# A gated attention and mixture-of-experts kernel: the running maximum is spread by transfers instead of matmuls, and two row normalizations change engine

## The reference, cut to what matters

```python
ig = (ifg @ igate_w.T + igate_b).T
fg = (ifg @ fgate_w.T + fgate_b).T
cs = jnp.cumsum(jax.nn.log_sigmoid(fg), axis=1)
log_D = jnp.where(tril, cs[:, :, None] - cs[:, None, :], -inf) + ig[:, None, :]
max_log_D = jnp.max(log_D, axis=-1, keepdims=True)
D_mat = jnp.exp(log_D - max_log_D)
C = einsum('hsd,htd->hst', qh, kh) / 8 * D_mat
normalizer = jnp.maximum(jnp.abs(C.sum(-1, keepdims=True)), jnp.exp(-max_log_D))
h = einsum('hst,htd->hsd', C / (normalizer + EPS), vh)
x = x + tanh(g_xattn[0]) * layernorm(h) * ln_scale
xn = layernorm(x)
top2 of softmax(xn @ router_w.T); y = weighted experts(xn); s = silu(xn @ sg) * (xn @ su) @ sd
x = x + tanh(g_ffn[0]) * (y + s)
```

## Time and profile before

| | us |
|---|---|
| runs (3) | 1070.31, 1074.41, 1075.37 |
| the profiled execution's own time | 1070.1 |
| its span, first to last instruction | 1068.5 |
| PE, DVE, ACT, POOL busy | 959.1, 807.3, 424.7, 419.4 |
| first stage, to the first expert tile | about 605 |
| mean granted TensorE clock | 0.956 |

### The profile page before, as it was taken

The page is one execution under the profiler, slowest core; times in us unless marked ns, Lnnn a source line. Parts: engine busy times, 40 slices in busy tenths (PEclk is TensorE's granted clock), DMA queues, the critical chain, the costliest instruction groups (busy, mean ns, idle before and its releaser), DMA issues.

```text
span 1068.5 us, 21065 instructions
## 1 busy us (share of the span) xinstructions
PE 959.1 (90%) x6143; PEld 804.3 (75%) x6143; DVE 807.3 (76%) x1995; ACT 424.7 (40%) x957; POOL 419.4 (39%) x315
## 2 busy tenths in 40 slices
PE   3689999999999998988998399999999999999982
PEld 2569888988898886977777278888888888677761
DVE  2887889888988989898866576666666666555885
ACT  2654445444544554444522134444444444332110
POOL 5010211221122122222123827668667777104775
PEclk9989999999999999999958699999999999999996
DMA  7570201220122022111004475576677674915888
GB/s 253 209 311 2 80 31 51 80 79 21 61 80 80 10 72 81 60 60 41 11 31 158 139 227 178 178 231 186 179 212 214 177 213 150 335 70 153 261 291 260
DMA packets 92778, 147.26 MB, mean 138 GB/s; under 512 B 10720, under 2 KB 51168, under 8 KB 91776
## 3 DMA queue, kind: packets, MB, share of 16 engines
q0 software_dynamic: 17872, 65.02, 18.8%
q1 hardware_dynamic: 62896, 59.79, 17.9%
q10 hardware_dynamic: 11904, 21.11, 5.6%
HBM read 89.26 MB, written 56.62 MB: 137 GB/s over the span
## 4 chain that ended last, share of the span: by engine, by line
PE 69%; DVE 13%; issue 7%; DMA 5%; POOL 4%; ACT 1%; SPq 1%; DVEq 0%; POOLq 0%; ACTq 0%
PE bank L1282 19%; PE bank L1152 13%; PE bank L1301 9%; PE bank L1165 5%; PE bank L1075 4%; POOL w_ring L699 3%; PE bank L1007 3%; PE bank L1096 2%; PE bank L1097 2%; PE bank L1349 2%; PE bank L1099 2%; DMA x2n<-routed_x 2%; PE bank L1292 2%; DMA base_out<-in_x_dram 2%; PE bank L1125 1%
## 5 line engine op out<-in xcount | busy, mean ns | idle before, releaser
L1282 PE MATMUL bank<-w_ring,x2nT 128*128 x948 | 254.3, 406 | 13.9 <-DVE x2nT L1864 13.6
L1282 PEld LDWEIGHTS bank<-w_ring,x2nT 128*128 128x128 f32 x948 | 173.8, 191 | 51.5 <-issue 15.8
L1152 PE MATMUL bank<-x2nT,w_ring 128*128 128x256 f32 x1152 | 149.8, 286 | 0.0
L580 POOL DMA_INDIRECT routed_x<-x2n,slot_u x64 | 65.8, 1029 | 204.4 <-DVE slot_u L1625 189.5
L1152 PEld LDWEIGHTS bank<-x2nT,w_ring 128*128 128x128 f32 x1152 | 142.3, 190 | 0.3
L1301 PE MATMUL bank<-w_ring,sh_actT 128*128 x474 | 121.2, 391 | 3.5 <-DVE sh_actT L1853 3.5
L1853 DVE TENSOR_TENSOR sh_actT<-bank,sh_actT 128x256 fp32r<-128x256 f32 x79 | 33.6, 425 | 108.9 <-ACT sh_actT L922 108.9
L1301 PEld LDWEIGHTS bank<-w_ring,sh_actT 128*128 128x128 f32 x474 | 88.8, 188 | 24.0 <-issue 4.6
L662 POOL TENSOR_TENSOR w_ring<-area,one 128x3072 fp32r<-128x3072 f32 x14 | 74.2, 5303 | 81.4 <-PE bank L1301 81.4
L699 POOL DMA_INDIRECT w_ring<-routed_y,y_slot x64 | 66.9, 1046 | 78.0 <-DMA routed_y<-cs_in 52.9
L665 POOL TENSOR_TENSOR w_ring<-area,w_ring 128x3072 fp32r<-128x3072 f32 x14 | 95.9, 6849 | 2.5 <-POOL w_ring L662 2.5
(11 more groups left out here) (224 smaller groups left out, 1959.1 us busy)
## 6 DMA issues: line engine op xcount, KB each, us to landing
x2n<-routed_x SPq DMA_DIRECT2D x316, 64.0 KB, 2.6
routed_y<-cs_in ACTq DMA_DIRECT2D x79, 256.0 KB, 3.3
base_out<-in_x_dram SPq DMA_DIRECT2D x16, 512.0 KB, 5.1
cs_in<-in_ctx_dram SPq DMA_DIRECT2D x16, 512.0 KB, 4.0
area<-n_L_ffn_expert_gate_dram POOLq DMA_DIRECT2D x16, 512.0 KB, 5.2
area<-in_L_ffn_expert_up_dram POOLq DMA_DIRECT2D x16, 512.0 KB, 6.9
area<-n_L_ffn_expert_down_dram POOLq DMA_DIRECT2D x16, 512.0 KB, 8.4
out_dram<-base_out SPq DMA_DIRECT2D x32, 256.0 KB, 3.8
```

Of the source, the lines that this page charges most:

```text
L580: pool.indirect_dma_start(out=routed_x, in_=x2n[:, b.par, j, :], in_offset=None, out_offset=bass.IndirectOffsetOnAxis(ap=slot_u[:, b.par, ...
L1152: last = mm(gu_bank(b.n, m)[:, at:at + S], w[:, w_part, c, m * P:(m + 1) * P], x2nT[:, x_part, c, :], start=(c + p == 0), stop=(c == DC - ...
L1282: last = mm(bank[2 + t.par][:, :], xtT[:, x_part, t.par, c * P:(c + 1) * P], w_gu[:, bass.ds(slot, 1), w_part, c, :].rearrange("p a i -> p ...
```

## The change

The maximum no longer passes through TensorE. SP writes `max_row` (8 rows of 256) to memory, and reads two heads' rows back into all 128 partitions of a new tile `max_spread` (two buffers of one pair each; the second block of 128 queries stands there twice, to be masked for the last 128 keys and left as it is for the first 128). POOL sets what lies above the diagonal to 1e30 by an `affine_select`, one for each pair of heads. ScalarE reads the exponential's input from `max_spread` instead of PSUM. `spread`, `max_hi`, the split in three parts and their constants go. The two banks MB become a second pair of score banks.

The normalized rows `xn` and `x2n` are made by ScalarE as `scale * x + shift` with two operands per partition; DVE makes the small tile of shifts (`-mean * rstd`) instead of the rows. In DVE's order `stats`, `top`, `choose`, `rank`, `slots` and `weigh` move; in PE's order the score pairs move ahead and `rank` behind. POOL's scatter moves behind the masks. The zeros and `kept_w` are written in 4 and 6 pieces of 1 MB from step 5 on, in between SP's other work. Constants and tables that are no longer needed go, and two small tables share another tile.

```diff
-        TP, SM, MB, QK, HO, FF = bank[0], bank[1], bank[2:4], bank[4:6], bank[6], bank[7]
+        TP, SM, QK, HO, FF = bank[0], bank[1], (bank[4:6], bank[2:4]), bank[6], bank[7]
...
+            def max_store(b):
+                sp.wait_ge(row_step.sem, row_step.upto(b.n, 4))
+                sp.dma_start(max_rows[b.par], max_row[:, :]).then_inc(max_out.sem, 16)
+
+            def max_load(b, q):
+                k, lap = q % 2, b.n * 2 + q // 2
+                sp.wait_ge(max_out.sem, max_out.upto(b.n))
+                sp.wait_ge(decay_made.sem, decay_made.upto(b.n, 2 * q - 2))
+                two = max_rows[b.par, 2 * q:2 * q + 2, :]
+                sp.dma_start(max_spread[:, k, 0:2 * ST, :].rearrange("p (h j) n -> p h (j n)", h=2),
+                             two.partition_broadcast(P)).then_inc(max_in[k].sem, 16)
+                sp.dma_start(max_spread[:, k, 2 * ST:, :], two[:, P:S].partition_broadcast(P)
+                             ).then_inc(max_in[k].sem, 16)
...
             for b in range(4, B):
-                if b == B // 2 - 2:
-                    sp.wait_ge(padded.sem, padded.upto(1))
+                if b == B - 3:
+                    sp.wait_ge(padded.sem, padded.upto(E // PADS))
+                max_back(Item(0, b - 3))
                 load_next(Item(0, b), more=b + 2 < B)
...
+                max_front(Item(0, b - 2))
+                if b >= B - 3:
+                    keep_w(b - B + 3)
...
+            def mask(b, q):
+                k, lap = q % 2, b.n * 2 + q // 2
+                pool.wait_ge(max_in[k].sem, max_in[k].upto(lap))
+                own = max_spread[:, k, 0:2 * ST, :]
+                g.affine_select(out=own, in_=own, compare_op=ALU.is_ge, fill=MASK, base=0,
+                                pattern=[[0, 2 * ST], [1, P]], channel_multiplier=-1).then_inc(max_masked.sem, 1)
...
                 if route:
                     h_stats(G)
+                if attend:
+                    mask(A, 2)
+                    mask(A, 3)
+                if front:
+                    values(F)
                 if route:
                     x2_stats(G)
+                if front:
+                    mask(F, 0)
+                    mask(F, 1)
+                if ahead:
+                    stats(N)
                 if rest and route:
                     scatter(H)
-                if front:
-                    values(F)
-                if ahead:
-                    stats(N)
...
+            def norm_front(b, j):
+                act.wait_ge(ln_shift_made.sem, ln_shift_made.upto(b.n))
+                act.wait_ge(xn_turned.sem, xn_turned.upto(b.n, j))
+                s.activation(xn[:, :], base_out[:, b.n * ST + j, :], ACT.Identity, bias=ln_shift[:, b.par, j:j + 1],
+                             scale=ln_rstd[:, b.par, j:j + 1]).then_inc(xn_made.sem, 1)
...
-                act.wait_ge(max_spread.sem, max_spread.upto(b.n, h + 1))
+                act.wait_ge(max_masked.sem, max_masked.upto(b.n * 4 + h // 2))
...
-                pe.wait_ge(c_made.sem, c_made.upto(b.n, 2 * q))
+                pe.wait_ge(c_made.sem, c_made.upto(b.n, 2 * q - 2))
...
-            def norm_front(b, j):
+            def front_shift(b):
                 dve.wait_ge(ln_rstd_made.sem, ln_rstd_made.upto(b.n))
...
+                v.scalar_tensor_tensor(ln_shift[:, b.par], ln_mv[:, b.par, :, 0], -1.0, ln_rstd[:, b.par],
+                                       ALU.mult, ALU.mult).then_inc(ln_shift_made.sem, 1)
...
-                dve.wait_ge(max_hi_made.sem, max_hi_made.upto(b.n))
-                v.tensor_tensor(max_rest[:, :], max_row[:, :], max_parts[0:NH, b.par, :], ALU.subtract
-                                ).then_inc(row_step.sem, 1)
```

201 lines of the change are left out of this document (98 added, 103 removed).

## The result

The changed kernel takes 1117.16 us in the median of 4 runs (1113.4 to 1118.58), the kernel before 1074.89 (4 runs on the same chip): a ratio of 1.0396, 95% interval 1.0356 to 1.0436. It is slower by 4%, where 1056 us, 1.7% faster, was forecast. The profiled execution took 1113.4 us, with a span of 1111.8.

A forecast was written before the change was run, and what follows sets the result against it. PE was taken to bound the eight full steps. Full steps -17.6, light steps +2.5, start +1 and end -2.5 us sum to -16.6: 1053.5 on the profiled execution, 1057.8 on the median, given as 1056, range 1047 to 1066 (overall 1036 to 1075).

The forecast's parts named there:

- the 33.1: Full step: what PE alone would need, 36.08 us less 2.5 for the spreads and 0.5 for a stall.
- a full step of 33.85: Forecast length of each full step: PE's 33.1 us plus 0.75 of waiting, a gain of 2.2.
- 0.75 us of waits: Full step: PE's waiting for ACT's normalizations at the turns of x tiles and x2n; bounds nothing and 2.8 us.
- the stall of 0.53 us: Full step: PE's stall before the second half of the shared MLP's last product, expected to go, gaining 0.5 us.
- the rival that was given 0.05: PE slows down: with more waiting PE gets clock 0.89 in full steps, 3.6 us a step back, 1080 us; chance 0.05.
- the term of +0.5 a step: Five light steps: each 0.5 us longer, 2.5 in all; bounds 3.4 us less to 2 more a step.
- The start: +1: Steps 0 and 1: first head 4.1 us later, 3 us of spreads saved on the path, together 1 later.
- The end: -2.5: Step 15: it loses its spreads on PE, 2.5 us less.
- The maximum comes late: Maximum's new way takes 10.5 us instead of 7.25, so heads wait for masks; slower, 1086 us; chance 0.11.
- point of decision at 9.5: Time from `max_row` to the mask's end, about 9.5 us, that decides whether the maximum comes late.
- GpSimd holds DVE up: POOL's four masks a step block DVE's instructions, 1.4 us a step over 13 steps, 18 lost, 1072 us; chance 0.09.
- PE runs free: Tiles always ready: full steps reach 33.1 us, light steps use 2 of DVE's 3.4 us, 1036 us; chance 0.15.

The follow-up runs named there:

- h1_best: Changed kernel with shared(G, 0) in bank TP, top(H) behind heads 6 and 7, GpSimd's queue in order of need, front_shift early: 1063.71 us, ratio 0.9904.
- h2_swap: Changed kernel with only the bank of shared(G, 0) exchanged, no engine's order moved: 1099.80 us, ratio 1.0256 to the kernel before.
- g3_swap: Changed kernel with shared(G, 0) in bank TP, scatter behind h_stats(G), x2_stats(G) ahead of mask(A, 3), top(H) behind heads 6 and 7: 1080.19 us, ratio 1.0088.
- h3_pool: Changed kernel with GpSimd's queue alone put in the order in which its results are wanted: 1110.06 us, ratio 1.0350 to the kernel before.
- i2_early: h1_best with the maximum's loads reading constant rows, so none waits for the maximum; attention's values left out: 1057.85 us, ratio 0.9833.

## Why the prediction was wrong

Of the 60 us between the forecast of the sum (16.6 less) and the span (43.3 more), the full steps have 28, the light ones 19, the start 10 and the end 4. No rival came near it: the slowest stood at 1086 us.

**What bounds, and PE's relief: right in kind.** PE loses the 32 matmuls, and once the other waits are gone PE bounds a full step of 33.07 us. That this is the 33.1 that "PE would need" is in part luck: the 33.1 has no waits in it, while PE stands 0.93 us in h1_best's step (0.75 were taken), and PE's busy time fell by 3.2 us, from 35.27 to 32.07, where 2.5 were taken for the spreads. The prices of the new operations were near: the mask 0.63 us (0.64), the loads 3.9 and 4.6 (the pair taken at 4.0), the way from `max_row`'s end to the first mask's end 6.9 us in step 7 (7.25).

**The step that failed is the one from PE's 33.1 us to a full step of 33.85.** It added 0.75 us of waits, for the turn of x2n and between the x tiles, and put every other wait of PE at nothing without a reason. The changed order gave PE one: `shared(G, 0)` waits for an addition on DVE that stands behind `rows`. The prediction counted the stall of 0.53 us in the earlier trace rows, which stands in PE's order ahead of that place, as gain and did not speak of the score pair that left it. It did not ask who used that time: DVE's addition did, with 0.5 us to spare. h2_swap, in which only the bank differs, puts the price at 2.1 of the 3.5 us by which a full step missed the 33.85. The other 1.4 went only in runs with several edits (34.05 in g3_swap, 33.07 in h1_best), so their cause is not shown by one; `top(H)` in front of the heads on ACT is the likely part. The slower clock, the mechanism of the rival that was given 0.05, lies in the 2.1 us: it came behind this wait and went with it.

**The light steps: the term of +0.5 a step should have been +4.3**, outside its bounds (-3.4 to +2). The text saw that the scatter "now waits behind the first two masks" and that the maximum comes about 1 us late, which was right. It did not go on to what stands behind the scatter in GpSimd's queue, `h_rstd`, for which DVE waits. h3_pool shows the queue's share as 1.4 of these 4.3 us in the mean, and up to 4.5 in one step. The rest went only with several edits together (32.10 in g3_swap, 31.41 in h1_best); the order on ACT and PE's slower clock are likely parts of it, and none is shown alone.

**The start: +1 should have been +11.** The 4.1 us for the first head were counted once, for step 0 (it waits 4.19), and set off against the spreads; the head of step 1, which waits 2.13, was not counted. Between `max_row` and the step that needs it lie only 2.5 us (step 0) and 4.6 us (step 1). PE's granted clock was 0.71 in step 1, where the kernel before had 0.88. i2_early shows what the lateness costs over the two steps with all that follows from it, 8.8 us in h1_best; for the changed kernel itself no run shows it.

**The end: -2.5 was +1.1.** From step 14's end to the first expert tile the changed kernel takes 71.7 us, the kernel before 71.9: the spreads of step 15 gave back almost nothing, and the cause stays open.

**The rivals.** "The maximum comes late" had the right sign, but not the cause: in full steps no first head waits, and in light ones the way takes 7.5 us, well under its point of decision at 9.5, and the first heads of steps 11 and 13 wait 0.8 and 0.6 us. "GpSimd holds DVE up" fell: of the operation of the earlier trace rows the median stayed at 0.415 us, the longest 0.778.

```profile
L1676 DVE SCALAR_TENSOR_TENSOR sh_actT<-sh_act,sh_actT x48: 407/415/778, 99.1 to 622.6; 128x256 fp32r<-128x256 f32 x48
```

"PE runs free" describes what the change can do in full steps when its queues are in order: h1_best's have its 33.1, but its light steps and its start do not follow.

## What to carry to other kernels

When work leaves the bounding engine, list for each instruction that moves up on it what it waits for, and where that stands in the other engine's order now: the time that left may have been somebody's cover. When an operation that waits for a transfer is put into an in-order queue, price every instruction behind it by who waits for that one, down to the smallest: here a power over 256 numbers ended 4.4 us later in its step than before, while a mask itself took 0.63. Here the exchanged bank took the wait away and the moved addition handed a part of it on, so look for a free buffer before moving an instruction.
